# Two small-head attention stages: a new order of the steps, the maximum subtracted in float32, and no products with zeros

## The chip, the cores and the metric

The kernel runs on one core of a Trainium2 chip. Its time is the device time of one execution in microseconds (us). A core has five engines, each with its own queue, which it works through in order: TensorE (PE; its weight loads are listed as PEld), VectorE (DVE), ScalarE (ACT), GpSimd (POOL) and SyncE (SP), which here only issues DMAs. Engines wait for one another by semaphores.

## The reference

A residual stream `x` of 64 batches x 128 tokens x 128 dimensions passes eight stages: four times a cross attention over a context of 77 tokens x 64 dimensions and then a feed-forward part, each gated by a tanh. The change touches the attention of the layers 0 and 2, which both have 16 heads of dimension 8. Layer 2, shortened (layer 0 is the same without the biases):

```python
qh = (q @ Wq + bq).reshape(B, LQ, HEADS, D_K).transpose(0, 2, 1, 3)      # HEADS = 16, D_K = 8
kh = (k @ Wk + bk).reshape(B, LKV, HEADS, D_K).transpose(0, 2, 1, 3)
vh = (v @ Wv + bv).reshape(B, LKV, HEADS, D_K).transpose(0, 2, 1, 3)
scores = jnp.einsum('bhqd,bhkd->bhqk', qh, kh) * scale
attn = jax.nn.softmax(scores, axis=-1)
out = jnp.einsum('bhqk,bhkd->bhqd', attn, vh)
concat = out.transpose(0, 2, 1, 3).reshape(B, LQ, D_MODEL)
return concat @ Wo + bo
...
x = x + jnp.tanh(g_xattn[2]) * _L2_xattn_ref(_layernorm(x, axis=-1), ctx_512, ctx_512, ...)
```

## The kernel before

The stages run one after another. Both small-head attention stages come from one function, `small_head_attention`; their tiles begin with `l0x_` and `l2x_`. `x` stays on the core (`x_res`), and all 64 batches are worked on there, in 16 iterations of four batches.

**What an iteration does once for its four batches** ("front" steps): statistics and normalization of `x` (DVE, with the inverse deviation on POOL), the transposes of `x` (PE, L362), queries (PE, L712), keys (PE, L717), and the values of two batches at a time (`values`, 40 products, PE, L735). All of them write to one PSUM bank, `pa`, so each waits until the one before has been read: the queries by ACT (a 16-bit high part) and DVE (the remainder), the values by DVE (`block_values`, L953), which masks them into blocks.

**What it does for each batch j.** The 16 heads of 77 keys make 1232 columns of scores, in four groups of four heads. Half A holds two groups, half B the other two. For each half: `score` (PE, L747; three 16-bit products for high and low parts, each on two row groups of 32 rows, which write to two banks), `maximum` over the 77 keys of each head (DVE, L961), `split_max` (POOL, L676 and L678: the maximum as a high and a low bfloat16 part), `turn_max` (PE, L754: heads become rows), `fetch_max` (ACT, L878), `shift` (PE, L763: a product with a matrix of -1 that subtracts the maximum inside PSUM), `exponential` (ACT, L885). Then the probabilities are turned in ten chunks of 128 columns, in three units (four, four and two chunks): `turn` (PE, L778), `high` (ACT, L891), `rest` (DVE, L965), `weigh` (PE, L797: three products a chunk with the values; between two chunks one product of 368 columns with a tile of zeros, L801, into unused columns of the same bank). At last `divide` (DVE, L973 and L977), `turn_o` (PE, L807), a copy (ACT, L897), `output` (PE, L811) and `add` into `x` (DVE, L985).

**What sets the order.** Every engine has its own list of steps, written out by hand as one string for each of the four batches (a "slot"), for instance on PE

```python
fronts = ["v1 x", "q", "k", "v0"]
... "scoreA turn0 turn_o scoreB output " + f + " mtA turn1 weigh0 shiftA mtB turn2 shiftB weigh1 weigh2"
```

Each name has a pair of numbers: a lag in iterations, and how many slots ago its batch began (`ago`). So in the slot in which the scores of batch j are made, the probabilities of batch j-1 are turned and weighed, and batch j-2 is divided, turned and added. `turn1` waits for `add` of the batch before, since the output is written into the bank that its transposes need (`turned[1]`).

Two constants are made by POOL in the first block, before any stage: `piece_mask`, and `minus_one` with 32 selects of 77 columns, each waiting for the one before (`make_attention_constants`, L518).

Of the kernel before, what the change touches and what calls it, by code (L numbers as in the profile page):

```python
# [14 lines left out]
F32 = mybir.dt.float32  # L15
# [7 lines left out]
P = 128  # L23
# [475 lines left out]
def make_attention_constants(pool, g, s_made):  # L499
# [32 lines left out]
CONSTANTS = 2 + 10 + 32 + 10  # L532


def small_head_attention(nc, g, name, wq, wk, wv, wo, bq=None, bk=None, bv=None, bo=None, gate=0):
# [17 lines left out]
    with Stage(nc, name) as st:  # L553
# [3 lines left out]
        four, none, blank = st.sb("four", [P, 4], F16), st.sb("none", [P, 2, 4]), st.sb("blank", [P, BANK], F16)  # L557
# [6 lines left out]
        mx, mh, mT = st.sb2("mx", [P, 4, 4]), st.sb2("mh", [P, 4, 32], BF16), st.sb2("mT", [P, P], BF16)  # L564
# [15 lines left out]
        s_score, s_max, s_mh, s_ml, s_mt, s_mT, s_shift, s_exp = [  # L580
            st.sem(k) for k in ("s_score", "s_max", "s_mh", "s_ml", "s_mt", "s_mT", "s_shift", "s_exp")]
# [26 lines left out]
        with nc.Block() as block:  # L608
# [18 lines left out]
            def _(pool):  # L627
                for i in range(2):
                    for p in range(2):
                        pool.memset(v_lo[p][i][:, :, :, D:E1], 0.0).then_inc(s_set, 1)  # L630
                    pool.memset(mh[i][:, :, :], 0.0).then_inc(s_set, 1)
                pool.memset(none[:, :, :], 0.0).then_inc(s_set, 1)
                pool.memset(blank[:, :], 0.0).then_inc(s_set, 1)
                pool.wait_ge(s_set, 8)
                pool.sem_inc(s_set, 1)

                def context_rest(it):
# [4 lines left out]
                    if (due := nth(it, 8, 3, ago=1)) is not None:  # L642
                        pool.wait_ge(s_ml, due)
# [24 lines left out]
                def split_max(it, j, h):  # L668

                    p = j % 2  # L670
                    pool.wait_ge(s_max, nth(it, 8, 2 * j + h))
                    if (due := nth(it, 8, 2 * j + h, back=4)) is not None:
                        pool.wait_ge(s_mt, due)
                    m = mx[p][:, 2 * h:2 * h + 2, :]
                    high, low = mh[p][:, 2 * h:2 * h + 2, 0:4], mh[p][:, 2 * h:2 * h + 2, 4:8]
                    pool.tensor_tensor(high, m, none[:, :, :], ALU.add).then_inc(s_mh, 1)  # L676
                    pool.wait_ge(s_mh, nth(it, 8, 2 * j + h))
                    pool.tensor_tensor(low, m, high, ALU.subtract).then_inc(s_ml, 1)  # L678
# [15 lines left out]
                steps.update(one)  # L694
# [133 lines left out]
            def _(act):  # L828
# [14 lines left out]
                def fetch_x(it):  # L843
                    fr.fetch(act, it, s_q)
# [2175 lines left out]
```

## Time and profile before

| | |
|---|---|
| median of 3 runs | 6037.49 us (6032.2 to 6039.96) |
| the profiled execution | 6016.21 us, its span 6014.5 us |
| mean granted TensorE clock | 0.916 of full speed |
| busy in the span: PE / DVE / ACT / POOL | 4935.3 / 3921.6 / 2728.1 / 2172.3 us |
| l0x: first and last scores | 41.2 and 636.4 us |
| l2x: first and last scores | 2583.4 and 3181.3 us |
| L801, products with zeros, l0x and l2x | 576 each, busy 160.9 and 162.9 us |

The profile is of one execution. A row of a timeline gives the start, the duration and the shape of an instruction, or of a few like ones that follow each other; in brackets stands how long the engine was idle before it and who released it. Durations of matmuls include the time that a result takes through the array, so that two which follow each other overlap: what one costs on the engine is read from start to start. The granted clock is in parts of 2.4 GHz, and 0.5 is 1.2 GHz.

### The profile page before, as it was taken

Reading aid. Unit: us, or ns where it says so; the run is one execution under the profiler, and the core shown is the slowest. Engines: PE = TensorE matmul, PEld = TensorE weight load, DVE = VectorE, ACT = ScalarE, POOL = GpSimd, SP = SyncE. Lnnn points to the kernel's source line nnn. Section 1 sums busy time; section 2 is a strip of 40 time slices with the busy share of each in tenths; the row PEclk is TensorE's granted clock in tenths of the full one; section 3 lists DMA queues with packets and bytes.
Section 4 is the critical chain, followed back from the end, with each engine's and each line's share of the span. In section 5 each row is a group of like instructions: output and inputs, shape, how many; then the busy total and the mean of one; then the engine's idle time right before and its main releaser. Section 6 shows DMA issues by size and latency. Waiting matters only on the chain. (4 is left out here: it accounts for less than half of the span.)

```text
span 6014.5 us, 133734 instructions
## 1 busy us (share of the span) xinstructions
PE 4935.3 (82%) x41787; PEld 3611.9 (60%) x41787; DVE 3921.6 (65%) x9897; ACT 2728.1 (45%) x5454; POOL 2172.3 (36%) x3095
## 2 busy tenths in 40 slices
PE   6888898999962798078888998888898799998888
PEld 3555466888862465045555665776776577776544
DVE  4555585777766333245555776888887688888544
ACT  3444475555530233044444554555554355554344
POOL 4333100111117100733332334777775733333300
PEclk9999798999985899579997998999999899999988
DMA  1000500000011333100000000000000000000000
GB/s 37 5 4 3 242 0 14 5 5 5 5 49 43 115 135 115 50 10 5 4 3 12 1 0 9 0 0 0 0 0 5 7 2 2 2 2 6 1 11 18
DMA packets 108942, 140.25 MB, mean 23 GB/s; under 512 B 35832, under 2 KB 83256, under 8 KB 103996
## 3 DMA queue, kind: packets, MB, share of 16 engines
q1 hardware_dynamic: 100544, 120.88, 6.0%
q0 software_dynamic: 8192, 16.79, 1.0%
q8 instruction: 109, 1.79, 0.1%
q14 instruction: 97, 0.79, 0.0%
HBM read 47.44 MB, written 58.72 MB: 18 GB/s over the span
## 5 line engine op out<-in xcount | busy, mean ns | idle before, releaser
L2170 POOL TENSOR_TENSOR l3a_probs<-l3a_probs,l3a_later 128x512 f32<-128x512 f32 x256 | 320.7, 1281 | 4.9 <-DVE l3a_total L2358 4.9
L2156 POOL TENSOR_TENSOR l3a_keys<-l3a_kT,head 128x2048 f32<-128x2048 f32 x64 | 230.4, 3600 | 232.8 <-ACT l3a_kT L2283 232.8
L1585 POOL DMA_INDIRECT l1c_rows<-l_rows,l1f_slots x128 | 123.1, 961 | 442.5 <-PEq L1577 402.0
L2218 PE MATMUL l3a_scores<-l3a_keys,l3a_qT 128*128 128x512 f32 x512 | 255.1, 601 | 4.2 <-POOL l3a_keys L2156 4.2
L170 POOL TENSOR_TENSOR l1x_ve<-l1x_mv,eps 128x1 f32<-128x1 f32 x64 | 12.2, 190 | 657.6 <-DVE l1x_mv L162 657.6
L965 DVE SCALAR_TENSOR_TENSOR l0x_p_lo<-l0x_turned,l0x_p_hi 128x512 f16<-128x512 f32 (+1 forms) x192 | 115.7, 603 | 204.4 <-ACT l0x_p_hi L891 202.2
L298 PE MATMUL l3a_po<-l3a_vals,l3a_probsT 128*128 128x32 f32 x2048 | 248.0, 269 | 0.2
L965 DVE SCALAR_TENSOR_TENSOR l2x_p_lo<-l2x_turned,l2x_p_hi 128x512 f16<-128x512 f32 (+1 forms) x192 | 115.7, 603 | 202.8 <-ACT l2x_p_hi L891 200.6
L298 PEld LDWEIGHTS l3a_po<-l3a_vals,l3a_probsT 128*128 128x128 f32 x2048 | 246.8, 192 | 0.7 <-ACT l3a_probsT L279 0.4
L1656 POOL TENSOR_TENSOR l2f_hid<-l2f_prod,l2f_route 128x512 f32<-128x512 f32 x128 | 152.1, 1193 | 257.0 <-DVE l2f_prod L1803 253.7
L254 ACT ACTIVATE l3a_probs<-l3a_probs 128x512 f32<-128x512 f32 x256 | 161.7, 632 | 182.4 <-DVE l3a_probs L245 177.2
L1504 PE MATMUL l1e_h<-l1e_xhi,l1f_parts 128*128 128x512 f16 x640 | 204.4, 380 | 9.7 <-DVE l1e_gated L1562 8.2
L2156 POOL TENSOR_TENSOR l3c_keys<-l3c_kT,head 128x1232 f32<-128x1232 f32 x64 | 144.0, 2250 | 159.9 <-ACT l3c_kT L2283 159.9
L284 DVE SCALAR_TENSOR_TENSOR l1x_loT<-l1x_turned,l1x_hiT 77x512 f16<-77x512 f32 x256 | 168.7, 679 | 46.9 <-ACT l1x_hiT L277 46.8
L277 ACT ACTIVATE l3c_hiT<-l3c_turned 77x512 f16<-77x512 f32 x256 | 150.5, 588 | 106.8 <-PE l3c_po L298 104.3
L1097 ACT ACTIVATE l0f_relu<-l0f_h,l0f_route 128x512 f32<-128x512 f32 x256 | 158.0, 687 | 83.6 <-DVE l0f_route L1136 44.2
L2218 PE MATMUL l3c_scores<-l3c_keys,l3c_qT 128*128 128x308 f32 x512 | 191.8, 457 | 1.0 <-POOL l3c_keys L2156 1.0
L284 DVE SCALAR_TENSOR_TENSOR l3c_loT<-l3c_turned,l3c_hiT 77x512 f16<-77x512 f32 x256 | 173.7, 679 | 20.3 <-ACT l3c_hiT L277 20.3
L1562 DVE TENSOR_TENSOR l1e_gated<-l1e_h,l1e_silu 128x512 f32<-128x512 f32 x160 | 110.7, 692 | 114.7 <-ACT l1e_silu L1536 114.7
L279 ACT COPY l3a_probsT<-l3a_turned 128x512 f32<-128x512 f32 x256 | 150.3, 587 | 77.1 <-PE l3a_turned L266 76.8
L277 ACT ACTIVATE l1x_hiT<-l1x_turned 77x512 f16<-77x512 f32 x256 | 144.8, 590 | 86.0 <-PE l1x_po L298 76.7
L237 DVE TENSOR_REDUCE l3a_mx<-l3a_scores 128x4 f32<-128x512 f32 x256 | 169.8, 684 | 21.1 <-issue 16.6
(581 smaller groups left out, 17374.6 us busy)
## 6 DMA issues: line engine op xcount, KB each, us to landing
l_rows<-l0f_zeros SPq DMA_DIRECT2D x34, 1024.0 KB, 26.2
l1f_parts<-l1f_split SPq DMA_DIRECT2D x40, 512.0 KB, 3.6
l1e_x_in<-l_rows SPq DMA_DIRECT2D x40, 256.0 KB, 2.8
l1f_down<-l1f_w SPq DMA_DIRECT2D x40, 256.0 KB, 2.3
l_rows<-l1e_y_out SPq DMA_DIRECT2D x40, 256.0 KB, 2.7
l1f_w<-in_L_W SPq DMA_DIRECT2D x16, 256.0 KB, 3.4
out_x<-x_res SPq DMA_DIRECT2D x16, 256.0 KB, 2.0
x_res<-in_x SPq DMA_DIRECT2D x1, 3840.0 KB, 12.2
```

The costliest lines, as they stand in the source:

```text
L237: dve.tensor_reduce(self.mx[it.par][:, a:b], self.view(c), AX, ALU.max).then_inc(self.s_max, 1)
L254: act.activation(v, v, ACT.Exp, scale=self.scale).then_inc(self.s_exp, 1)
L277: act.activation(self.hiT[c % 2][:, :], src, ACT.Copy, scale=SPLIT_EXP).then_inc(self.s_fetch, 1)
L284: dve.scalar_tensor_tensor(self.loT[c % 2][:, :], self.ps_turn[c % 2][0:self.keys, :], SPLIT_EXP, self.hiT[c % 2][:, :], ALU.mult, ALU.sub ...
L298: last = pe.matmul(out_of(h), p[c % 2][:, cols], v, start=(i == 0), stop=(i == len(products) - 1))
L965: dve.scalar_tensor_tensor(p_lo[u][:, :], turned[u % 2][:, 0:len(UNITS[u]) * P], SPLIT_EXP, p_hi[u][:, :], ALU.mult, ALU.subtract).then_in ...
L1097: act.activation(relu[e][:, :], ps_h[e][:, :], ACT.Relu, scale=rt.w[it.par][:, j, e:e + 1]).then_inc(s_relu, 1)
L1504: last = pe.matmul(bank[:, :], parts[p][:, w, f], x[p][:, :], start=(k == 0), stop=(k == 2))
L1656: pool.tensor_tensor(hid[k % 2][:, :].rearrange("p (e m) -> p e m", m=M), prod[k % 2][:, :].rearrange("p (e m) -> p e m", m=M), rt.w[it.pa ...
L2156: pool.tensor_tensor(keys[it.par][:, :, :, :], kT[it.par][:, :, :].unsqueeze(2).to_broadcast([P, J, G4, T]), g.head32[:, :].unsqueeze(1).u ...
L2170: pool.tensor_tensor(v, v, later[:, :].unsqueeze(1).to_broadcast([P, 4, T]), ALU.mult).then_inc(s_masked, 1)
L2218: pe.matmul(scores[c][:, 0:G4 * T], qT[it.par][:, c, :], keys[it.par][:, c, :, :].rearrange("p h t -> p (h t)"), start=True, stop=True).th ...
```

## The change

- **Order.** A batch now takes two slots and no third: the transposes of its first unit stand in the slot of its scores (`turn0`, `ago` 0), its other units, the division, `turn_o`, `output` and `add` in the next one (`ago` 1). The front steps move to the slot's end, and the second values block (`v1`) to the middle of the fourth slot, before `turn_o`; the transposes of `x` stand at that slot's end, and some front steps run one iteration earlier than before.
- **Maximum.** `split_max` goes. DVE writes the maximum into a float32 tile of 32 columns a group, whose others are zero; `turn_max` and `shift` are float32 products, and `mT` and `minus_one` are float32.
- **Zeros.** The products with zeros (L801) and their tile go.
- **Constants.** `minus_one` needs 16 selects in place of 32, and both constants are made in the block of l0x, by POOL, after it has cleared its tiles. A copy of the identity in bfloat16 goes.

```diff
-    for k in range(8):
-        part, j = k // 4, k % 4
+    for j in range(4):
         v = g.minus_one[:, j, :]
         for q in range(4):
-            pool.affine_select(out=v, in_=v, compare_op=ALU.not_equal, fill=-1.0, base=-(32 * q + 4 * part + j),
+            pool.affine_select(out=v, in_=v, compare_op=ALU.not_equal, fill=-1.0, base=-(32 * q + j),
...
-        mx, mh, mT = st.sb2("mx", [P, 4, 4]), st.sb2("mh", [P, 4, 32], BF16), st.sb2("mT", [P, P], BF16)
+        mx, mT = st.sb2("mx", [P, 4, 32]), st.sb2("mT", [P, P])
...
+                if first_use:
+                    make_attention_constants(pool, g, g.s_made)
...
-                def split_max(it, j, h):
...
-                skewed(pool, n, slots(steps, ["maxA value1 maxB s1", "maxA maxB rest s2 " + ("bias" if biased else ""),
-                                              "maxA maxB deviation s3", "maxA maxB next value0"]), 6)
+                skewed(pool, n, slots(steps, ["s1 value0", "deviation s2 value1", "s3 " + ("bias" if biased else ""), "next rest"]), 6)
...
-                    pe.wait_ge(s_ml, nth(it, 8, 2 * j + h))
-                    pe.matmul(scores[h][64 * h:64 * h + 64, W + 12:W + 12 + P], mh[j % 2][:, 2 * h:2 * h + 2, :].rearrange("p g r -> p (g r)"),
-                              g.ident16[:, :], start=False, stop=True, skip_group_check=True).then_inc(s_mt, 1)
+                    pe.wait_ge(s_max, nth(it, 8, 2 * j + h))
+                    pe.matmul(scores[h][64 * h:64 * h + 64, W + 12:W + 12 + P], mx[j % 2][:, 2 * h:2 * h + 2, :].rearrange("p g r -> p (g r)"),
+                              g.ident[:, :], start=False, stop=True, skip_group_check=True).then_inc(s_mt, 1)
...
-                        if c < 9:
-
-                            pe.matmul(po[:, HEADS * E1:BANK], blank[:, 0:P], blank[:, HEADS * E1:BANK], start=False, stop=False,
-                                      skip_group_check=True)
...
-                    steps[f"turn{u}"] = (lambda it, j, u=u: turn(it, j, u), 2, 1)
+                    steps[f"turn{u}"] = (lambda it, j, u=u: turn(it, j, u), 2, 1 if u else 0)
                     steps[f"weigh{u}"] = (lambda it, j, u=u: weigh(it, j, u), 2, 1)
-                fronts = ["v1 x", "q", "k", "v0"]
-                skewed(pe, n, slots(steps, ["scoreA turn0 turn_o scoreB output " + f + " mtA turn1 weigh0 shiftA mtB turn2 shiftB weigh1 weigh2"
-                                            for f in fronts]), 6)
+                fronts = [("", "q"), ("", "k"), ("", "v0"), ("v1", "x")]
+                skewed(pe, n, slots(steps, ["scoreA turn1 turn2 weigh0 mtA weigh1 shiftA weigh2 scoreB turn0 " + mid +
+                                            " turn_o mtB output shiftB " + end for mid, end in fronts]), 6)
...
-                fronts = ["v1 x", "c q", "k", "v0"]
-                skewed(act, n, slots(steps, ["o high0 " + f + " mA high1 expA mB high2 expB" for f in fronts]), 6)
+                fronts = [("x", "v0"), ("q", "v1"), ("k", ""), ("", "c")]
+                skewed(act, n, slots(steps, [begin + " high1 high2 mA expA " + mid + " high0 o mB expB" for begin, mid in fronts]), 6)
...
-                dve.tensor_reduce(mx[j % 2][:, 2 * h:2 * h + 2, :], half(h), AX, ALU.max).then_inc(s_max, 1)
+                dve.tensor_reduce(mx[j % 2][:, 2 * h:2 * h + 2, 0:4], half(h), AX, ALU.max).then_inc(s_max, 1)
...
-                fronts = ["norm v1", "q", "k stats", "v0"]
-                skewed(dve, n, slots(steps, ["divide maxA rest0 maxB add " + f + " rest1 rest2" for f in fronts]), 6)
+                fronts = [("", "", "stats"), ("q", "", "norm"), ("k", "", ""), ("v0", "v1", "")]
+                skewed(dve, n, slots(steps, ["maxA rest1 rest2 " + begin + " maxB divide rest0 " + mid + " add " + end
+                                             for begin, mid, end in fronts]), 6)
```

On PE, before the change, the second half of a slot of l0x with the keys, from the output product to the second subtraction (`mh` is the split maximum, `mT` the turned one, `po` the weighed values):

```order
L811 MATMUL l0x_turned<-l0x_wo,l0x_oT 128x128 [waits l0x_s_oT]
L717 MATMUL l0x_pa<-l0x_ctx,l0x_wk 128x308 [waits l0x_s_qlo,l0x_s_ctx0]
L754 MATMUL l0x_scores<-ident,l0x_mh 64x128 [waits l0x_s_ml]
L778 MATMUL l0x_turned<-ident,l0x_probs 128x128 [waits l0x_s_x,l0x_s_exp]
...
L797 MATMUL l0x_po<-l0x_v_hi,l0x_p_hi 128x18 [waits l0x_s_o,l0x_s_vlo,l0x_s_lo]
...
L801 MATMUL l0x_po<-l0x_blank 128x368
...
L763 MATMUL l0x_scores<-minus_one,l0x_mT 128x308 [waits l0x_s_mT]
L763 MATMUL l0x_scores<-minus_one,l0x_mT 128x308
L754 MATMUL l0x_scores<-ident,l0x_mh 64x128 [waits l0x_s_ml]
L778 MATMUL l0x_turned<-ident,l0x_probs 128x128 [waits l0x_s_lo,l0x_s_exp]
...
L763 MATMUL l0x_scores<-minus_one,l0x_mT 128x308 [waits l0x_s_mT]
```

After it, PE in the corresponding stretch, from the scores of half B to the keys at the slot's end (`mx` is the maximum in float32, `o` the divided result):

```order
L730 MATMUL l0x_scores<-l0x_keys_hi,l0x_q_hi 128x308 [waits l0x_s_exp,l0x_s_keys]
...
L761 MATMUL l0x_turned<-ident,l0x_probs 128x128 [waits l0x_s_lo,l0x_s_exp]
...
L786 MATMUL l0x_turned<-ident,l0x_o 128x128 [waits l0x_s_o]
L737 MATMUL l0x_scores<-ident,l0x_mx 64x128 [waits l0x_s_max]
L790 MATMUL l0x_turned<-l0x_wo,l0x_oT 128x128 [waits l0x_s_oT]
L746 MATMUL l0x_scores<-minus_one,l0x_mT 128x308 [waits l0x_s_mT]
L746 MATMUL l0x_scores<-minus_one,l0x_mT 128x308
L700 MATMUL l0x_pa<-l0x_ctx,l0x_wk 128x308 [waits l0x_s_qlo,l0x_s_ctx0]
```

The division's transpose and the output have moved between the two halves' subtractions, the keys behind the second one, and the turned maximum waits for VectorE itself (`s_max`) and no longer for GpSimd (`s_ml`).

On DVE, before the change, one slot with the keys (`mx` maximum, `p_lo` remainder of the probabilities, `recip` and `o` the division):

```order
L973 RECIPROCAL l0x_recip<-l0x_po 128x16 [waits l0x_s_o,l0x_s_weigh]
L977 TENSOR_TENSOR l0x_o<-l0x_po,l0x_recip 128x128 [waits l0x_s_oTp,l0x_s_recip]
L961 TENSOR_REDUCE l0x_mx<-l0x_scores 128x8 [waits l0x_s_ml,l0x_s_score]
L965 SCALAR_TENSOR_TENSOR l0x_p_lo<-l0x_turned,l0x_p_hi 128x512 [waits l0x_s_hi]
L961 TENSOR_REDUCE l0x_mx<-l0x_scores 128x8 [waits l0x_s_ml,l0x_s_score]
L985 SCALAR_TENSOR_TENSOR x_res<-l0x_turned,gates,x_res 128x128 [waits l0x_s_y]
L944 TENSOR_TENSOR l0x_k_lo<-l0x_pa,l0x_k_hi 128x308 [waits l0x_s_khi]
```

And after it, the slot that takes up the keys:

```order
L942 TENSOR_REDUCE l0x_mx<-l0x_scores 128x2x4 [waits l0x_s_mt,l0x_s_score]
L946 SCALAR_TENSOR_TENSOR l0x_p_lo<-l0x_turned,l0x_p_hi 128x512 [waits l0x_s_hi]
L946 SCALAR_TENSOR_TENSOR l0x_p_lo<-l0x_turned,l0x_p_hi 128x256 [waits l0x_s_hi]
L923 TENSOR_TENSOR l0x_k_lo<-l0x_pa,l0x_k_hi 128x308 [waits l0x_s_khi]
L942 TENSOR_REDUCE l0x_mx<-l0x_scores 128x2x4 [waits l0x_s_mt,l0x_s_score]
L954 RECIPROCAL l0x_recip<-l0x_po 128x16 [waits l0x_s_o,l0x_s_weigh]
L958 TENSOR_TENSOR l0x_o<-l0x_po,l0x_recip 128x128 [waits l0x_s_oTp,l0x_s_recip]
L946 SCALAR_TENSOR_TENSOR l0x_p_lo<-l0x_turned,l0x_p_hi 128x512 [waits l0x_s_hi]
L966 SCALAR_TENSOR_TENSOR x_res<-l0x_turned,gates,x_res 128x128 [waits l0x_s_y]
```

The division stood ahead of both maxima and now stands behind the second.

## Rows read from the trace of the kernel before

**Rows 1.** Windows: length; busy us of PE, PEld, DVE, ACT, POOL; granted clock; DMA; GB/s.

```profile
315.07:352.35 37.28, 30.58 (x373) 19.72 (x370) 20.76 (x50) 17.61 (x38) 13.68 (x29) 0.95 0.02 4
...
308.60:312.00 3.40, 3.40 (x25) 2.31 (x24) 0.57 (x1) 1.59 (x4) 2.74 (x5) 0.54 0.00 0
...
609.00:636.00 27.00, 25.03 (x176) 13.74 (x175) 9.67 (x20) 8.37 (x19) 5.00 (x14) 0.50 0.00 1
```

**Rows 2.** Timeline, PE, one slot: start, duration, what, [idle before <- releaser].

```profile
315.07 0.30 PE L747 MATMUL l0x_scores<-l0x_keys_hi,l0x_q_hi 32*128 32x308 f16 x2
...
315.57 0.66 PE L778 MATMUL l0x_turned<-ident,l0x_probs 128*128 128x128 f32 x4
...
316.76 0.49 PE L811 MATMUL l0x_turned<-l0x_wo,l0x_oT 128*128 128x128 f32 x2
317.08 1.02 PE L712 MATMUL l0x_pa<-l0x_xT,l0x_wq 128*128 128x512 f32 x2
318.04 0.24 PE L754 MATMUL l0x_scores<-ident,l0x_mh 128*64 128x128 bf16 x1
318.97 0.63 PE L778 MATMUL l0x_turned<-ident,l0x_probs 128*128 128x128 f32 x4 [0.69 <-DVE x_res L985]
...
321.83 0.30 PE L763 MATMUL l0x_scores<-minus_one,l0x_mT 32*128 32x308 bf16 x2 [0.53 <-ACT l0x_mT L878]
...
323.39 0.30 PE L747 MATMUL l0x_scores<-l0x_keys_hi,l0x_q_hi 32*128 32x308 f16 x2
```

**Rows 3.** Timeline, PE, end of the iteration's fourth slot.

```profile
345.63 0.93 PE L362 MATMUL l0x_pa<-ident,l0x_xn 128*128 128x128 f32 x4 [2.37 <-DVE l0x_v_f L953]
...
352.35 0.30 PE L747 MATMUL l0x_scores<-l0x_keys_hi,l0x_q_hi 32*128 32x308 f16 x2
```

**Rows 4.** Timeline, DVE, the slot of rows 2.

```profile
315.18 0.26 DVE L973 RECIPROCAL l0x_recip<-l0x_po 128x16 f32<-128x16 f32 x1 [0.86 <-PE l0x_po L797]
315.47 0.29 DVE L977 TENSOR_TENSOR l0x_o<-l0x_po,l0x_recip 128x128 f32<-128x128 f32 x1
315.76 0.80 DVE L961 TENSOR_REDUCE l0x_mx<-l0x_scores 128x8 f32<-128x616 f32 x1
...
320.34 0.69 DVE L965 SCALAR_TENSOR_TENSOR l0x_p_lo<-l0x_turned,l0x_p_hi 128x512 f16<-128x512 f32 x1 [0.81 <-ACT l0x_p_hi L891]
```

**Rows 5.** Timeline, POOL, the slot of rows 2.

```profile
316.73 0.20 POOL L676 TENSOR_TENSOR l0x_mh<-l0x_mx,l0x_none 128x8 bf16<-128x8 f32 x1 [4.90 <-DVE l0x_mx L961]
317.00 0.20 POOL L678 TENSOR_TENSOR l0x_mh<-l0x_mx,l0x_mh 128x8 bf16<-128x8 f32 x1
```

**Rows 6.** Timeline, ACT, the slot of rows 2.

```profile
319.71 0.60 ACT L891 ACTIVATE l0x_p_hi<-l0x_turned 128x512 f16<-128x512 f32 x1 [0.75 <-PE l0x_turned L778]
...
321.51 0.26 ACT L878 CAST l0x_mT<-l0x_scores 64x128 bf16<-64x128 f32 x1
...
322.17 0.68 ACT L885 ACTIVATE l0x_probs<-l0x_scores 128x616 f32<-128x616 f32 x1
```

**Rows 7.** Timeline, PE, weighing: a zero product and what follows.

```profile
319.51 0.32 PE L801 MATMUL l0x_po<-l0x_blank 128*128 128x368 f16 x1
319.67 0.17 PE L797 MATMUL l0x_po<-l0x_v_hi,l0x_p_hi 128*128 128x27 f16 x1
319.69 0.17 PE L797 MATMUL l0x_po<-l0x_v_lo,l0x_p_hi 128*128 128x27 f16 x1
```

**Rows 8.** Timeline, PE, two float32 products of 308 columns, elsewhere.

```profile
325.50 0.78 PE L717 MATMUL l0x_pa<-l0x_ctx,l0x_wk 64*128 64x308 f32 x2
...
4855.05 0.68 PE L2218 MATMUL l3c_scores<-l3c_keys,l3c_qT 128*128 128x308 f32 x2
```

**Rows 9.** Timeline, ACT and POOL, start of the kernel.

```profile
4.34 0.21 ACT L2911 ACTIVATE gates<-gates_in 128x8 f32<-128x8 f32 x1 [2.24 <-DMA gates_in<-in_g_ffn]
4.85 6.22 POOL L518 TENSOR_SCALAR_AFFINE_SELECT minus_one<-minus_one 128x77 bf16<-128x77 bf16 x16
...
26.88 0.20 POOL L339 TENSOR_TENSOR l0x_ve<-l0x_mv,eps 128x4 f32<-128x4 f32 x1 [4.75 <-DVE l0x_mv L329]
```

More of the change, by code:

```diff
@@ L529, in make_attention_constants @@
     return n
-CONSTANTS = 2 + 10 + 32 + 10
+CONSTANTS = 2 + 10 + 16 + 10
 def small_head_attention(nc, g, name, wq, wk, wv, wo, bq=None, bk=None, bv=None, bo=None, gate=0):
@@ L556, in small_head_attention @@
         bqkv_s, bo_s, bvo_s = st.sb("bqkv", [P, 3]), st.sb("bo", [P, P]), st.sb("bvo", [P, P])
-        four, none, blank = st.sb("four", [P, 4], F16), st.sb("none", [P, 2, 4]), st.sb("blank", [P, BANK], F16)
+        four = st.sb("four", [P, 4], F16)
         ctx2, ctxT = st.sb2("ctx2", [P, GROUP, KEYS]), st.sb2("ctxT", [P, GROUP, 3, KEYS], F16)
@@ L641, in context_rest @@
                     pool.wait_ge(fr.s_rstd, nth(it))
-                    if (due := nth(it, 8, 3, ago=1)) is not None:
-                        pool.wait_ge(s_ml, due)
+                    if (due := nth(it, 4, 0, ago=1)) is not None:
+                        pool.wait_ge(s_keys, due)
                     lo = ctxT[p][CTX:P, :, :, :]
@@ L666, in value_rest @@
                                        ALU.subtract).then_inc(s_vlo, 1)
-                def split_max(it, j, h):
[L670 to L678, printed above, removed]
                 def add_bias(it):
@@ L686, in add_bias @@
                     pool.tensor_tensor(x, x, bvo_s[:, :].unsqueeze(1).to_broadcast([P, GROUP, P]), ALU.add).then_inc(s_bo, 1)
-                steps = {"maxA": (lambda it, j: split_max(it, j, 0), 2, 0), "maxB": (lambda it, j: split_max(it, j, 1), 2, 0)}
-                one = {"deviation": (lambda it, j: fr.inverse_deviation(pool, it), 0, 0), "rest": (lambda it, j: context_rest(it), 1, 0),
-                       "bias": (lambda it, j: add_bias(it), 1, 0), "value0": (lambda it, j: value_rest(it, 0), 1, 0),
+                steps = {"deviation": (lambda it, j: fr.inverse_deviation(pool, it), 0, 0), "rest": (lambda it, j: context_rest(it), 0, 0),
+                       "bias": (lambda it, j: add_bias(it), 1, 0), "value0": (lambda it, j: value_rest(it, 0), 2, 0),
                        "value1": (lambda it, j: value_rest(it, 1), 2, 0), "next": (lambda it, j: spread(it, 0), 1, 0),
@@ L811, in output @@
                     pe.matmul(y_p, oT[j % 2][:, :], wo_s[:, :], start=True, stop=True).then_inc(s_y, 1)
-                steps = {"x": (lambda it, j: turn_x(it), 1, 0), "q": (lambda it, j: queries(it), 1, 0), "k": (lambda it, j: keys_of(it), 1, 0),
-                         "v0": (lambda it, j: values(it, 0), 1, 0), "v1": (lambda it, j: values(it, 1), 2, 0),
-                         "turn_o": (turn_o, 2, 2), "output": (output, 2, 2)}
+                steps = {"x": (lambda it, j: turn_x(it), 0, 0), "q": (lambda it, j: queries(it), 1, 0), "k": (lambda it, j: keys_of(it), 1, 0),
+                         "v0": (lambda it, j: values(it, 0), 1, 0), "v1": (lambda it, j: values(it, 1), 1, 0),
+                         "turn_o": (turn_o, 2, 1), "output": (output, 2, 1)}
                 for h, half_name in enumerate("AB"):
@@ L905, in _ @@
                 for u in range(3):
-                    steps[f"high{u}"] = (lambda it, j, u=u: high(it, j, u), 2, 1)
-                fronts = ["v1 x", "c q", "k", "v0"]
-                skewed(act, n, slots(steps, ["o high0 " + f + " mA high1 expA mB high2 expB" for f in fronts]), 6)
+                    steps[f"high{u}"] = (lambda it, j, u=u: high(it, j, u), 2, 1 if u else 0)
+                fronts = [("x", "v0"), ("q", "v1"), ("k", ""), ("", "c")]
+                skewed(act, n, slots(steps, [begin + " high1 high2 mA expA " + mid + " high0 o mB expB" for begin, mid in fronts]), 6)
             @block.vector
```

34 lines of the change are left out of this document (14 added, 20 removed).

## The prediction

> **What bounds the kernel now.** I read the page's table of slices first, then the windows of one iteration, then the timelines of the four engines for one slot. The change touches only the two small-head attention stages, l0x and l2x. Each walks 64 batches in groups of four; a batch is one slot of the order, and four slots make an iteration. One iteration of l0x takes 37.28 us, in which TensorE is busy 30.58, VectorE 20.76, ScalarE 17.61 and GpSimd 13.68 [rows 1]. No engine is full: TensorE is nearest, but a good part of its time is the products with zeros and pipeline overlap. What sets the slot is therefore a ring of hand-overs, and the PE timeline of a slot shows it [rows 2]: scores of one half at 315.07, transposes of the previous batch, output, query product at 317.08, the turned maximum at 318.04, then 0.69 us of idleness until VectorE's residual add lets the transposes at 318.97 go, later 0.53 us for the maximum copied by ScalarE, and the next slot at 323.39: 8.32 us. Three slots of an iteration are like that, the fourth is longer: from the row at 345.63, where TensorE has just stood idle 2.37 us for the value products to leave the shared bank, to the next slot at 352.35 [rows 3]; 37.28 less three times about 8.35 leaves 12.2 us for it. That hole has a second price: right behind the same hole of the iteration before, from 308.60 to 312.00, the granted clock is 0.54, against 0.95 over a whole iteration [rows 1], so the work behind the hole runs at the lower of the two levels, 1.2 and not 2.4 GHz.
>
> Between score and subtraction a half passes VectorE (maximum 0.80 us [rows 4]), GpSimd (two instructions of 0.20, 0.27 apart [rows 5]), TensorE (0.24 [rows 2]), ScalarE (0.26 [rows 6]) and TensorE again (0.30 [rows 2]).
>
> **Part 1, products with zeros.** Nine go per batch. One moves the next product on by 0.16 us, from 319.51 to 319.67, and a value product moves it by 0.02 to 0.03 [rows 7]. So 9 x 0.16 = 1.4 us per slot leave TensorE. In the old order they stand between the wait and the next slot, so they are on its ring; this is the surest gain, 1.4 x 128 slots = 180 us if nothing took its place. The float32 steps below take most of it.
>
> **Part 2, the maximum in float32.** GpSimd's two steps go, 0.20 + 0.27 and a hand-over, some 0.5 us per half. In their place the turn becomes a float32 product of 128 columns: the output product has this form and takes 0.49 us for its two instructions [rows 2], against 0.24, so +0.25. The subtraction is the term that decides. Now two products of 308 columns in different row groups finish together in 0.30 us [rows 2]. In float32 each is two instructions; the nearest rows are a float32 pair of 308 columns on 64 rows, 0.78 us, and one on the whole array, 0.68 [rows 8]. No row has two of them in neighbouring row groups. Lower bound: they overlap wholly, 0.70 us. Upper bound: one after the other, 1.2 to 1.4 us. Since a product's two instructions are issued one behind the other in the same row group, only the second of the first product can run beside the first of the second product, which makes three instructions' time in place of four: 3 x 0.26 and some 0.12 for entering the 32-row form. I take 0.90 us of issue. There are 256 such steps (2 halves x 128 batches), so 0.1 us on each is 26 us of the total.
>
> The Trainium skill ("TensorE: Matmul & The Clock Gate", Part 3) says that products in distinct row groups run concurrently, about 4 ns apart. The trace agrees for 16-bit operands (the 0.30 above). By that rule read for whole products the step would be 0.70; read for instructions in program order, 0.90. No run here shows it for float32.
>
> **Part 3, the order.** I lay out a new slot by its order, with the rows' durations. Scores A: 0.50 (315.07 to 315.57 [rows 2]). The second chunk of the previous batch is then turned, copied high, subtracted and weighed: 0.66 for four transposes [rows 2], 0.63 from the copy's start to the remainder's, 0.69 for the remainder [rows 4, 6], with 0.12 of hand-overs 2.10. Beside it lie the third chunk's transposes, the first chunk's weighing, the maximum of half A (0.80, ready 1.5 us into the slot) and its turn: they cost nothing, but that stands on the 2.10; without this cover the maximum's way would be 0.80 + 0.49 + 0.26. Weighing chunk 1: 12 products, 0.31. Subtraction A: 0.90. Weighing chunk 2: 0.15. Scores B until VectorE can start, 0.61, and their maximum, 0.80; the division that is now queued behind that maximum on VectorE: 0.58 (0.26 and 0.29 with a gap [rows 4]); hand-over 0.10; together 2.10. The exponential of A (0.68 [rows 6]) and the transposes of chunk 0 lie beside this. Turning o 0.15, turning maximum B 0.49, its copy 0.26, hand-overs 0.12: 1.02. Subtraction B: 0.90. Sum 0.50 + 2.10 + 0.31 + 0.90 + 0.15 + 2.10 + 1.02 + 0.90 = 7.98 us. Behind it comes the slot's front step: queries 0.96 (317.08 to 318.04 [rows 2]), keys 0.70 (0.78 [rows 8] less the end that overlaps), values 40 x 0.026 = 1.04, and in the last slot the transposes of x, 0.50, with about 0.25 more for the second values block, of whose 1.04 the rest fits into the wait for the division. The front also hides the exponential of B: 0.90 + 0.96 + 0.50 is longer than the way from subtraction B through 0.68 us of exponential.
>
> So the four slots are 8.94, 8.68, 9.02 and 8.73: 35.4 us against 37.28. The three ordinary slots get longer by 0.5 (the ring now holds two subtractions in float32 and the division behind a maximum), the long one shorter by 3.5: the wait for the values bank goes, since the second values block stands early in its slot with three steps between it and x's transposes, and with it the spell of low clock. 1.9 us x 32 iterations = 61 us. Other edits cost nothing: GpSimd's queue is shorter by 16 short steps an iteration, so each wait that it served ends no later; the ScalarE copy of the maximum has the same size; the context load keeps two iterations of lead.
>
> **Part 4, the start.** Sixteen of the 32 selects that make the constants go. Sixteen take 6.22 us [rows 9]. The rest moves from the first block into l0x, ahead of GpSimd's first work on the deviation, which now starts at 26.88 [rows 9]. The first block then lasts only until the gates are made, 4.55 [rows 9], and what leaving it takes, an estimated 6 us; clearing takes about 2; of the constants 6.2 for the sixteen selects and an estimated 3.5 for the others remain (in float32, which I take to cost the same). So GpSimd is free at about 17.7, and the weights, now requested while the large load of x is under way, land at about the same time. Gain 9 us, between 6 (only the selects) and 12.
>
> **The sum.** 61 + 9 = 70 us off the profiled execution's 6016.2 us (span 6014.5 and 1.7 around it): 5946. The median of the runs is 6037.5, 21 above; with the same 70 it becomes 5967 us.
>
> **Rivals.**
> A. The two subtractions overlap wholly (0.70): 0.2 x 256 = 51 us more, 5916; with looser hand-overs than I reckon, down to 5870. For it: 16-bit products do overlap [rows 2]. Against: the issue order within a product. Chance 0.22.
> B. They do not overlap (1.2 to 1.4): 84 us or more are lost, 6050 to 6095, no change or slightly slower. For it: float32 on 64 rows already takes 0.10 more than on the whole array [rows 8]. Chance 0.14.
> C. The slower side: the clock. Without zero products the ordinary slots have thinner work, and if TensorE is granted 1.2 GHz there, its terms on the path double: scores 1.0, first transposes 0.5, weighing 0.46, subtractions 1.8, turn 0.3, front 0.85, that is 4.9 us per slot, 627 us if it held for all 128. The point from which it decides is a ninth of the slots beyond what runs low today; at a third of the slots the time is about 5967 + 209 = 6176. For it: the last 27 us of l0x, which have no front steps but still the zero products, run at 0.50 clock [rows 1]. Against: today's falls follow a hole of 2.4 us, and the longest wait that I find in the new slot is 0.8; and the float32 turns and subtractions put back 0.25 and 0.6 us of work per half, more than the 1.4 us of zeros per slot. Chance 0.13.
> The Trainium skill (same page, Part 4) says that transposes do not count as busy for the clock gate. By that rule only the stretch between scores A and subtraction A would be thin, which is rival C.
>
> **How the numbers follow.** Forecast 0.51, its own range 5925 to 6010; A 0.22; B 0.14; C 0.13. A measurement of this kernel can tell about 0.2%, 12 us, from no change. Faster by more: forecast, A and a little of B, 0.77. Within 0.2%: a part of B, 0.07. Slower: the rest of B and C, 0.16. The range takes in A and the lower end of B: 5855 to 6055.
>
> **What would show it.** Right: an iteration of about 35.4 us with four nearly equal slots; no idleness over 1 us before the transposes of x; subtraction steps at a pace of 0.9; the first deviation at 18 us; clock at or above 0.95 in both stages. Wrong: a step of 0.70 or 1.2 in its place (A, B), VectorE's division no longer the last thing before o's turn, a granted clock of 0.5 over whole slots (C), or a wait of TensorE for GpSimd's keys.

## The result and the profile after

The changed kernel takes 6371.4 us (median; 6370.8 to 6376.8) against 6037.6 (6032.2 to 6040.0): a ratio of 1.055, 95% interval 1.0534 to 1.0566. It is slower by 334 us where 70 fewer were forecast; 404 us lie between, about two thirds of the 627 that rival C, the clock, had for all slots. Rival C is what happened.

The page of the changed kernel: span, busy times, and TensorE's granted clock in 40 slices.

```profile
span 6369.6 us, 131931 instructions
PE 5431.0 (85%) x41403; PEld 3838.7 (60%) x41403; DVE 3933.8 (62%) x9897; ACT 2733.7 (43%) x5454; POOL 2067.6 (32%) x2562
PEclk8555589899995799555555799999999899999978
```

The two groups of fives are the two stages. Windows of the changed kernel, with the columns of [rows 1]: a slot, four slots, and most of each stage.

```profile
314.89:327.33 12.44, 12.39 (x114) 7.80 (x112) 5.38 (x12) 4.47 (x9) 3.22 (x3) 0.50 0.01 1
302.87:351.56 48.69, 46.63 (x358) 26.77 (x358) 20.95 (x50) 17.89 (x38) 10.57 (x13) 0.54 0.02 4
100.00:600.00 500.00, 483.16 (x3599) 276.12 (x3599) 213.69 (x510) 182.32 (x388) 108.15 (x133) 0.52 0.02 4
2800.00:3300.00 500.00, 484.01 (x3654) 277.11 (x3650) 215.73 (x510) 184.32 (x388) 121.28 (x143) 0.51 0.02 4
```

An iteration takes 48.69 us where [rows 1] has 37.28 and the forecast 35.4. TensorE is busy 46.63 us of it and is now the bound, at 1.2 GHz: the ring of hand-overs has become a full engine. (48.69 - 37.28) x 32 = 365 us, and the start gives 6 back: about the 355 us by which the spans of the two profiled executions differ (6369.6 and 6014.5). The timeline of PE shows one slot, and in the next one a short return to 2.4 GHz.

```profile
327.33 0.44 PE L730 MATMUL l0x_scores<-l0x_keys_hi,l0x_q_hi 32*128 32x308 f16 x2
...
330.00 0.69 PE L737 MATMUL l0x_scores<-ident,l0x_mx 128*64 128x128 f32 x2
...
331.25 1.39 PE L746 MATMUL l0x_scores<-minus_one,l0x_mT 32*128 32x308 f32 x4
332.58 0.20 PE L780 MATMUL l0x_po<-l0x_v_hi,l0x_p_hi 128*128 128x18 f16 x1
...
333.72 1.11 PE L761 MATMUL l0x_turned<-ident,l0x_probs 128*128 128x128 f32 x4
335.26 0.48 PE L786 MATMUL l0x_turned<-ident,l0x_o 128*128 128x128 f32 x1 [0.43 <-DVE l0x_o L958]
335.67 0.69 PE L737 MATMUL l0x_scores<-ident,l0x_mx 128*64 128x128 f32 x2
336.29 0.80 PE L790 MATMUL l0x_turned<-l0x_wo,l0x_oT 128*128 128x128 f32 x2
337.02 1.40 PE L746 MATMUL l0x_scores<-minus_one,l0x_mT 32*128 32x308 f32 x4
338.35 2.08 PE L695 MATMUL l0x_pa<-l0x_xT,l0x_wq 128*128 128x512 f32 x2
340.35 0.44 PE L730 MATMUL l0x_scores<-l0x_keys_hi,l0x_q_hi 32*128 32x308 f16 x2
...
343.01 0.43 PE L737 MATMUL l0x_scores<-ident,l0x_mx 128*64 128x128 f32 x2
...
344.24 0.79 PE L746 MATMUL l0x_scores<-minus_one,l0x_mT 32*128 32x308 f32 x4
344.96 0.18 PE L780 MATMUL l0x_po<-l0x_v_hi,l0x_p_hi 128*128 128x18 f16 x1
...
347.15 0.48 PE L786 MATMUL l0x_turned<-ident,l0x_o 128*128 128x128 f32 x1 [0.61 <-DVE l0x_o L958]
```

The start of one instruction to the start of the next is its pace. A subtraction has 1.33 us (331.25 to 332.58) at 1.2 GHz and 0.72 (344.24 to 344.96) at 2.4; queries 2.00 (338.35 to 340.35) where [rows 2] has 0.96. The longest wait in this piece is 0.61 us, for the division; from 100 to 600 us it is 0.7 (us in all, times, longest):

```profile
PE l0x_turned L786 <- DVE l0x_o L958: 11.9, 31, 0.7
```

So the clock lies at 1.2 GHz although TensorE is 96% busy and never waits 1 us.

### The profile page after: what moved, and what is told of

Read it like the earlier page. It is cut to its first block and busy times, and to the rows that moved or that the text cites. A ratio compares the mean times of both kernels' runs of the same rounds, so it can differ in the third digit from the quotient of the medians.

```text
span 6369.6 us, 131931 instructions
## 1 busy us (share of the span) xinstructions
PE 5431.0 (85%) x41403; PEld 3838.7 (60%) x41403; DVE 3933.8 (62%) x9897; ACT 2733.7 (43%) x5454; POOL 2067.6 (32%) x2562
## 5 line engine op out<-in xcount | busy, mean ns | idle before, releaser
L942 DVE TENSOR_REDUCE l0x_mx<-l0x_scores 128x8 f32<-128x616 f32 x128 | 102.4, 800 | 306.7 <-PE l0x_scores L730 306.7
L942 DVE TENSOR_REDUCE l2x_mx<-l2x_scores 128x8 f32<-128x616 f32 x128 | 102.4, 800 | 302.2 <-PE l2x_scores L730 302.2
L864 ACT ACTIVATE l0x_probs<-l0x_scores 128x616 f32<-128x616 f32 x128 | 87.5, 683 | 217.1 <-PE l0x_scores L746 217.1
## 6 DMA issues: line engine op xcount, KB each, us to landing
x_res<-in_x SPq DMA_DIRECT2D x1, 3840.0 KB, 12.4
```

The source lines that it names most:

```text
L942: dve.tensor_reduce(mx[j % 2][:, 2 * h:2 * h + 2, 0:4], half(h), AX, ALU.max).then_inc(s_max, 1)
```

## The experiments

The ratio is to runs of the kernel before on the same chip, and its interval is 0.1 to 0.4% to either side; times of different chips are compared by the ratios where it matters. "Clock" is the granted clock from 100 to 600 us, inside l0x. "Split" is the maximum as two bfloat16 parts made by GpSimd, as before; "direct" one bfloat16 value written by VectorE.

| run | order | maximum | zeros in weighing | in the wait | us | ratio | clock |
|---|---|---|---|---|---|---|---|
| before | old | split | 9 | 0 | 6037.6 | 1 | 0.94 |
| e2 | old | split | 0 | 0 | 6073.3 | 1.0071 | 0.59 |
| e6 | old | split | 9, on 32 rows | 0 | 6581.7 | 1.0922 | 0.55 |
| e4 | new | split | 9 | 0 | 6028.7 | 0.9986 | 0.87 |
| e5 | new | split | 0 | 0 | 6104.9 | 1.0129 | 0.52 |
| e3 | old | float32 | 9 | 0 | 6238.7 | 1.0346 | 0.89 |
| e16 | old | float32 | 0 | 0 | 6211.1 | 1.0287 | 0.62 |
| e1 | new | float32 | 9 | 0 | 6216.5 | 1.0301 | 0.83 |
| after | new | float32 | 0 | 0 | 6371.4 | 1.0550 | 0.52 |
| e7 | new | float32 turn, bfloat16 subtraction | 0 | 0 | 6103.2 | 1.0130 | 0.54 |
| e9 | new | float32 | 9 | 4 | 6089.4 | 1.0067 | 0.97 |
| e10 | new | float32 | 0 | 4 | 6134.7 | 1.0134 | 0.69 |
| e14 | new | float32 | 0 | 4, on 32 rows | 6510.9 | 1.0774 | 0.51 |
| e13 | old | direct | 9 | 0 | 6027.4 | 0.9986 | 0.93 |
| e8 | new | direct | 9 | 0 | 6002.0 | 0.9955 | 0.86 |
| e11 | new | direct | 9 | 4 | 5933.6 | 0.9808 | 0.97 |
| e12 | new | direct | 0 | 4 | 6029.2 | 0.9979 | 0.70 |
| e15 | new | direct | 5 | 5 | 5891.0 | 0.9750 | 0.95 |

### Three parts, one at a time (e1 to e5, e16)

**e1**: the changed kernel with the zero products back in `weigh`.

```diff
+                        if c < 9:
+                            pe.matmul(po[:, HEADS * E1:BANK], blank[:, 0:P], blank[:, HEADS * E1:BANK], start=False, stop=False, ...)
```

> The changed kernel with the products with zeros put back between the chunks, nothing else. Theory 1 (clock: the zeros held TensorE's clock up): granted clock in both stages back to 0.9 or more, an iteration of 36 to 39 us instead of 48.7, time 6000 to 6100 us. Theory 2 (float32: the turn and the subtraction in float32 are too long for the ring, whatever the clock): the zeros only add 1.4 us a slot, time 6400 us or more, clock as low as in the changed kernel.

**e2**: the kernel before without these two lines.

> The kernel before without the products with zeros, nothing else. Theory 1: the clock falls to 0.5 for most of both stages and the slots go from 8.3 to 10 us or more, time above 6200 us. Theory 2: the ring gets shorter by 1.4 us a slot, 1.4 x 128 = 180 us, time about 5860 us, clock above 0.85 there.

**e3**: the old order and its zeros, the maximum in float32 (`mx`, `mT`, `minus_one` and the turn as in the change, and the constants made in l0x).

> The old order with the products with zeros, but with the float32 maximum (no GpSimd step, float32 turn and subtraction) and the constants made in l0x. Theory 1: clock at 0.9 or more in both stages; on the ring 2 x (0.25 + 0.6) are added and 2 x 0.5 go, about 0.7 us a slot, 6037 + 90 - 6 = 6120 us. Theory 2: 6300 us or more.

**e4**: the new order with the zeros and `split_max` of before. The constants are made in l0x, but with all 32 selects, so nothing is gained at the start (first scores at 41.6 us).

> The new order with the old maximum (split by GpSimd, bfloat16 turn and subtraction) and with the products with zeros. Theory 1: clock 0.9 or more, the ring is that of e1 less the float32 parts (2 x 0.85) plus GpSimd (2 x 0.5), an iteration of 34 to 37 us, time 5930 to 6040 us. Theory 3 (the order itself is what is longer, since the division stands behind the second maximum): 6050 us or more at a clock of 0.9.

**e5**: e4 without the zeros.

> The new order, with the maximum split into two bfloat16 parts by GpSimd as before and without the products with zeros. It completes the square of order, type of the maximum, and zeros. Theory 1 (taking the zeros out costs through the clock, by an amount that grows with the float32 work that then runs at 1.2 GHz): 6029 for the new order with zeros, plus about the 34 us that their removal cost in the old order: 6055 to 6090, stage clock 0.55 to 0.65. Rival 1 (the new order itself is too thin for the clock, the type does not matter): plus the 155 us of the float32 pair, about 6180. Rival 2 (in the new order the zeros are on the ring and their 1.4 us a slot come back): below 5950.

**e16**: e3 without the zeros.

> The old order with the maximum in float32 and without zeros: the missing corner. If type and zeros are all (float32 subtractions on 32 rows do not hold the clock and take 1.33 us at 1.2 GHz against 0.37): 6239 with zeros plus about the same 155 as in the new order: 6340 to 6420, stage clock 0.50 to 0.55. Rival (the new order makes the fall, the old one keeps 1.0 in its ordinary slots as with bfloat16): 6239 + 35 = 6260 to 6290.

With the zeros in, the order is worth -9 us (split) and -22 (float32), and float32 costs 201 (old) and 188 (new). The -9 is not clear of nothing: e4's interval is 0.9973 to 1.0. Taking the zeros out costs 36 and 76 with the split maximum (43 and 86 by the ratios), but -28 in the old order and +155 in the new one with float32 (-36 and +150 by the ratios; the -36 has an interval of some 29 to either side).

Of the expectations only e4's was met, and its clock, 0.87, was under the 0.9 expected. e1 (6216) and e2 (6073) fell between their two theories, e3 (6239) between its 6120 and its 6300, and e5 (6105, clock 0.52) between 6090 and its rival's 6180. In e2 the clock did fall as theory 1 had it, to 0.59, but the time rose by 36 us only. The parts do not add: in e16 I expected 6340 to 6420 and its rival 6260 to 6290, and both failed. One thing in e3 explains a piece of it. The waits of PE there, from 100 to 600 us:

```profile
PE l0x_scores L731 <- issue: 15.4, 8, 3.1
```

Eight stops of up to 3.1 us in which nothing that the profile shows is awaited; neither the kernel before nor e16 has such a row among its waits there. Over two stages of 700 us that is some 40 us of e3's 6239, and more with the fall of the clock behind them: a slot of 9.3 us without a stop lasts 12.4 to 13.7 with one. What these stops are was not tried. Without them, taking the zeros out would cost the old order some 12 us or more in place of saving 28, and in the new order it costs 155. The clock says the same: without zeros it is 0.59 and 0.62 in the old order, 0.52 in the new one, with either type.

### Turn or subtraction (e7)

```diff
-        mx, mT = st.sb2("mx", [P, 4, 32]), st.sb2("mT", [P, P])
+        mx, mT = st.sb2("mx", [P, 4, 32]), st.sb2("mT", [P, P], BF16)
```

and `minus_one` in bfloat16.

> The changed kernel with its products with zeros back, the turn of the maximum in float32, but the turned maximum copied and subtracted as one bfloat16 product. Theory (the float32 steps cost what they add to TensorE's work, since with zeros TensorE is nearly full): the turn adds 0.25 us and the subtraction 0.45 to each of 256 halves, so of the 187 us between the split bfloat16 maximum (6029) and float32 (6216) some 64 stay: 6029 + 64 = 6093, less up to 30 if GpSimd's two steps were on the ring; 6060 to 6100. Rival (it is the turn, with its two loads of a weight that was just written, that costs): about 6200. Rival (only the clock matters and 16-bit subtractions keep it): 6030 or less.

This text says that the zeros are back, but the kernel that ran has none, so its expectation was not put to the test, and it stands beside e5 and the changed kernel. 6103.2 against 6104.9: a float32 turn without GpSimd's two steps costs what the split cost, within the 6 us by which e7's first scores come earlier (35.6 and 41.6). All that lies between e7 and the changed kernel, 268 us (254 by the ratios), is the subtraction in float32, at nearly the same clock (0.54 and 0.52): 256 steps x (1.33 - 0.37) = 246 us, with 0.37 us as the pace of the bfloat16 one in e7 at 1.2 GHz (both rows are of e7, timeline of PE):

```profile
300.77 0.44 PE L746 MATMUL l0x_scores<-minus_one,l0x_mT 32*128 32x308 bf16 x2
301.14 1.39 PE L700 MATMUL l0x_pa<-l0x_ctx,l0x_wk 64*128 64x308 f32 x2
```

### What holds the clock (e6, e9, e10, e14)

**e6**: the kernel before, its zeros on 32 rows.

```diff
-  pe.matmul(po[:, HEADS * E1:BANK], blank[:, 0:P], blank[:, HEADS * E1:BANK], ...)
+  pe.matmul(po[:, HEADS * E1:BANK], blank[0:32, 0:P], blank[0:32, HEADS * E1:BANK], ...)
```

> The kernel before, with its products with zeros on 32 rows of the array in place of 128; same count, columns and places in the order. If what holds the clock is that TensorE is streaming, whatever the rows: the time of before, 6025 to 6050, clock 0.91. If rows in use count, the zeros on 32 rows hold it no better than none: clock near 0.85 as without zeros, and since their 1.4 us a slot are still spent and at the lower clock count double, 6150 to 6300.

The clock fell from 0.94 to 0.55 with the same number of columns streamed, so it is not streaming as such that holds it. The time went beyond my range, since a product on 32 rows between products on 128 costs more than its columns. A chunk (three value products, one of zeros) of e6:

```profile
304.37 0.22 PE L797 MATMUL l0x_po<-l0x_v_hi,l0x_p_hi 128*128 128x18 f16 x1
304.44 0.18 PE L797 MATMUL l0x_po<-l0x_v_lo,l0x_p_hi 128*128 128x18 f16 x1
304.47 0.17 PE L797 MATMUL l0x_po<-l0x_v_hi,l0x_p_lo 128*128 128x18 f16 x1
304.57 0.48 PE L801 MATMUL l0x_po<-l0x_blank 32*128 32x368 f16 x1
304.99 0.20 PE L797 MATMUL l0x_po<-l0x_v_hi,l0x_p_hi 128*128 128x27 f16 x1
```

0.62 us (304.37 to 304.99), where the same chunk of the kernel before in its spell at 1.2 GHz has 0.39:

```profile
310.56 0.22 PE L797 MATMUL l0x_po<-l0x_v_hi,l0x_p_hi 128*128 128x18 f16 x1
310.69 0.47 PE L801 MATMUL l0x_po<-l0x_blank 128*128 128x368 f16 x1
310.95 0.23 PE L797 MATMUL l0x_po<-l0x_v_hi,l0x_p_hi 128*128 128x27 f16 x1
```

0.23 x 9 x 128 = 265 us of e6 are that.

**e9, e10 and e14** put four zero products where TensorE waits for the division (0.43 to 0.80 us), into a bank that is free then: e9 on top of e1, e10 on the changed kernel alone, e14 as e10 with `blank[0:32, ...]`.

```diff
                 def turn_o(it, j):
+                    for _ in range(4):
+                        pe.matmul(turned[1][:, 0:368], blank[:, 0:P], blank[:, 0:368], start=True, stop=True)
                     pe.wait_ge(s_o, nth(it, 4, j))
```

> The new order with float32 maximum and its products with zeros back, and four more products with zeros (128 rows, 368 columns, 0.16 us each at 2.4 GHz) placed where TensorE waits 0.8 us for the division, before the turn of o. They write a part of a PSUM bank that is free then. Theory (the clock is the cause of the slots beyond 9.17 us, and it is held by products on all 128 rows): the granted clock in the stages rises from 0.83 towards 0.95, an iteration comes to 4 x 9.2 = 37 us in place of 43, and the time to 6010 to 6060. Rival (TensorE was full, so more products only lengthen the ring): 6216 plus 4 x 0.16 x 128 = 82 at most, 6220 to 6300.

> The changed kernel as it is, with only the four products with zeros in the wait before the turn of o, none among the value products. If four such products in the wait are enough to keep 2.4 GHz, the layout of the forecast can be read: an iteration of 35.4 to 36.5 us and a time of 5965 to 6010. If they are not enough, they cost at 1.2 GHz 4 x 0.31 less the wait of 0.5: about 0.7 us a slot, 6371 + 90 = 6460; between the two if the clock comes back for some slots. I expect the latter, 6200 to 6460, since 0.65 us of them is less than half the 1.4 us that were taken out.

> The kernel of the run with four zeros in the wait alone (6135; the changed kernel 6371), with these four on 32 rows in place of 128: same columns, same place. If any streaming holds the clock: 6120 to 6160, stage clock 0.69 to 0.74. If only rows in use count: the clock stays at 0.50 to 0.53 and the four cost what they take beyond the wait at 1.2 GHz, 6420 to 6500.

Work added, time gone: e1 6216 to e9 6089, the changed kernel 6371 to e10 6135. On 32 rows the same four cost 376 us more than on 128. None of the three expectations was met in time. e9 is 29 us above its range; its stops of up to 3.1 us with no releaser, 11.8 and 11.0 us in 500 us of either stage, are about that much. e10 is faster than the 6200 that I had as its lower end. e14 is 11 us above 6500, since the four took 1.34 us with the change from and to products on 128 rows, where I had 1.24, and filled a wait of 0.29 us a slot on average (11.9 us in 500 us of the changed kernel), where I had 0.5. PE windows (length, PE busy, granted clock, DMA share, GB/s) from 100 to 600 us, of e10 (the profiled execution took 6210 us, where three of its five took 6121 to 6135), then of e14:

```profile
100.00:600.00 500.00, 480.17 (x4162) 0.69 0.02 4
```

```profile
100.00:600.00 500.00, 495.62 (x3471) 0.51 0.02 4
```

e14 is the busier of the two and stays at 1.2 GHz. In this kernel four products a slot on all 128 rows raise the clock; the same products on 32 rows do not. It fits that the float32 subtractions, 0.72 us of 32-row products per half, did not stand in for the zeros: e7, which has them in bfloat16, has 0.54 where the changed kernel has 0.52.

### Towards a better version (e8, e11, e12, e13, e15)

**e8**: the new order with zeros, and VectorE writes the maximum straight as bfloat16. The same rounded value is subtracted from all keys of a query and head, so it cancels in the softmax.

```diff
-        mx, mT = st.sb2("mx", [P, 4, 32]), st.sb2("mT", [P, P])
+        mx, mT = st.sb2("mx", [P, 4, 32], BF16), st.sb2("mT", [P, P], BF16)
```

> The new order with zeros; VectorE writes the maximum straight as one bfloat16 value, GpSimd takes no part, turn and subtraction stay in bfloat16. The same value is subtracted from all keys of a query and head, so it cancels in the softmax. If GpSimd's two steps and hand-overs (0.5 us a half) are on the ring of the new order: up to 0.5 x 256 = 128 us below the 6029 of the same order with the split: 5900 to 5960. If they lie beside TensorE's other work: 6010 to 6030.

**e11**: e8 with the four products in the wait. **e12**: e11 without the zeros in `weigh`. **e13**: e8's edit in the old order. **e15**: e11 with `if c < 9 and c % 2 == 0` (five zeros in weighing) and `range(5)`.

> The new order, the maximum as one bfloat16 value without GpSimd, the zeros among the value products, and the four in the wait before the turn of o. Without the four, slots at a clock of 1.00 last 8.22 to 8.74 us and the slots with the keys and the values 10.9 at 0.69. Theory (the fill holds the clock through those): 34 us an iteration against 37, 3 x 32 = 96 below 6002: 5890 to 5930, stage clock 0.95 or more. Rival (the spell at 1.2 GHz comes from the keys' float32 product on 64 rows, not from the wait): no change or slower, 6000 to 6060.

> The same with the four in the wait alone, none among the value products. Where the wait is the thin place, the clock holds and the 1.4 us a slot are gone from the ring: 5850 to 5890. Where the amount over the slot counts, four are too few for nine: stage clock 0.5 to 0.7 and 6050 to 6120, as the same order without zeros (6105).

> The old order with its zeros, the maximum as one bfloat16 value written by VectorE, no GpSimd step (constants made in l0x as in the changed kernel). In the old order TensorE waits some 0.5 us for the turned maximum, behind GpSimd's two steps. If that wait goes with them, without another in its place: 0.3 to 0.5 us in half of the steps, 40 to 60 us, and 6 of the start: 5975 to 5995, as good as the new order (6002), so that the order is worth nothing. Rival (the ring in the old order runs over the residual add, not the maximum): 6020 to 6040, and the direct maximum pays only in the new order.

> The best version so far (5934) with five zeros among the value products in place of nine, and five in the wait in place of four. If the wait was the thin place, the clock stays at 0.95 or more and some 0.6 us a slot less stand on TensorE, of which about half on the ring: 0.3 x 128 = 40 us, 5890 to 5910. If the amount over the slot counts: stage clock 0.8 to 0.9 and 5960 to 6010.

GpSimd's two steps lie beside other work: nothing measurable in the old order (e13, interval 0.997 to 1.0003, as its rival had it), 0.3% in the new one (e8 against e4, each by its ratio), of which 6 us, a third, is the earlier start (first scores at 35.7 and 41.6 us). e8 fell between its two ranges. The four in the wait bring 68 us (e8 to e11; 89 by the ratios), 4 us above the range, at the clock expected. In e12 the four alone do not suffice (clock 0.70, and 6029 us, between its two ranges). e15 is the best kernel here: 0.975 of before, interval 0.973 to 0.9769, as its first theory had it. PE windows by slot, from one turn of o to the next, of e11 and of e15:

```profile
338.63:347.92 9.29, 9.01 (x154) 1.00 0.00 0
347.92:356.06 8.14, 7.67 (x80) 1.00 0.00 0
356.06:364.73 8.67, 8.13 (x77) 1.00 0.00 0
364.73:373.04 8.31, 7.78 (x77) 1.00 0.08 19
```

```profile
301.72:309.62 7.90, 7.18 (x77) 1.00 0.00 0
309.62:318.04 8.42, 7.64 (x75) 1.00 0.00 0
318.04:326.03 7.99, 7.29 (x74) 1.00 0.08 20
326.03:335.96 9.93, 9.75 (x152) 0.83 0.00 0
```

34.4 us in e11's iteration and 34.2 in e15's, against 37.28. At the same clock four zeros fewer in weighing (one more in the wait) shorten a slot by 0.24 to 0.32 us, about half of their 0.64. In the iteration of e15 shown here the slot with both value blocks falls to 0.83 and gives most of that back. In about half of e15's iterations it does not fall and lasts 9.1 us, and over l0x, from the first scores to the last, e15 takes 532 us and e11 552; l2x gives 22 us more, together about the 43 us between the two runs.

The place counts beside the number, as e15 and e8 suggest: ten zero products a slot, five of them in the wait, give a clock of 0.95, and nine, none in the wait, give 0.86. No run adds four elsewhere than in the wait, so how much is due to the place is not shown.

## Why the prediction was wrong

**The step that failed** is the weighing of rival C: "the float32 turns and subtractions put back 0.25 and 0.6 us of work per half, more than the 1.4 us of zeros per slot". I counted busy time. The larger part, the subtractions, are products on 32 rows, and e14 against e10 shows that such products do not hold the clock (0.51 against 0.69); of what was put back only the turns' 0.25 us run on 128 rows. For the same reason part 1 priced the zeros at 1.4 us per slot and at nothing otherwise. My other argument against C, that a fall needs a long wait, was wrong too: the fall in the kernel before does follow a hole of 2.4 us [rows 3], but the clock of the changed kernel is 0.50 over whole slots, and its longest wait from 100 to 600 us is 0.7 us. The row that spoke for C, the last 27 us of l0x at 0.50 with TensorE 25.03 us busy [rows 1], was the one to follow: busy and slow at once. And once TensorE is full, the price is no longer the terms on the ring but all its work. C's 4.9 us per slot was an overestimate all the same: an iteration is longer than the forecast by 13.3 us, 3.3 a slot. Of the 1.6 us between, 0.9 is the subtraction, which C doubles from 0.90 to 1.80 us where it takes 1.33, twice a slot; the rest was not taken apart.

How the 404 us between forecast and result divide, two experiments show: with the zeros back (e1) 155 us go, and with the clock at 0.97 (e9) another 127. The 122 us left down to the forecast's 5967 are about what nine zero products a slot make at half their time (0.7 us x 128 = 90) with e9's stops (some 29).

**Part 1.** Removal at a constant clock is worth half its time (e11, e15), not 1.4 us per slot. With what the clock does, removal costs 36 to 155 us except in the old order with float32.

**Part 2.** The turn: 0.43 us in its row against 0.24, forecast +0.25; about right in size, and nearly free (e7). The subtraction: 0.72 at 2.4 GHz, not 0.90. Rival A's number, 0.70, was right and my argument from the issue order wrong: both pairs overlap. (The prediction's 0.12 for entering the 32-row form has no row there; 2 x 0.72 - 1.33 = 0.11 is the part of the step that does not grow when the clock halves.) GpSimd's 0.5 us per half was off the ring. The sum does not rest on it, but my expectations of e3 and e4 gave credit for it, wrongly. At a clock of 1.00, float32 makes slots of

```profile
307.80:316.94 9.14, 8.94 (x87) 1.00 0.00 0
316.94:326.57 9.63, 9.46 (x82) 1.00 0.01 2
326.57:335.88 9.31, 9.06 (x82) 1.00 0.10 19
```

(e9, PE windows) against 8.14, 8.67 and 8.31 for the same slots of e11: 1.0 us more per slot. Neither kernel has GpSimd's steps, so my terms make 2 x (0.25 + 0.60) = 1.7 us; the step was 0.49 us longer than in bfloat16 and not 0.60: 0.72 against 0.23 from start to start, the latter from 321.83 [rows 2] to

```profile
322.06 0.19 PE L797 MATMUL l0x_po<-l0x_v_hi,l0x_p_hi 128*128 128x27 f16 x1
```

How much of the rest lay beside waits was not taken apart.

**Part 3.** The layout was near. e9's three slots and the one before them, with both value blocks,

```profile
297.52:307.80 10.28, 10.28 (x160) 1.00 0.01 3
```

make an iteration of 38.4 us (297.52 to 335.88). Take half of nine zeros from each (0.7 us): 35.6, against 35.4 forecast. This is worked out; no run shows the order with float32, no zeros and a full clock. The nearest, e10, has iterations in l0x from 37.5 us, at clocks of 0.84 to 1.00, to 47.9. The wait for the values bank did go, and with it the hole. What the layout missed is that a gain of the order holds only at 2.4 GHz: with zeros in weighing alone the order brings 0.14%, at a clock of 0.87 (e4). That it is its own wait for the division which lets the clock sink is likely, since zeros put there bring it back (e8 to e11), but not shown apart from their number. The division was the last thing before o's turn, as forecast.

**Part 4.** GpSimd starts on l0x at 6.04 us and on the deviation at 18.25, as forecast (18). But the first scores come at 35.5 in place of 41.2: 5.7 us, just under the range of 6 to 12. In the old order with the same constants (e3, e13) they come at 32.5, 8.7 us earlier: the constants gave the 9 us, and the new order's own start takes 3 of them back.

**Still open:** why without zeros the old order holds 0.59 to 0.62 and the new one 0.52. The new order sets transposes and weighing, the 128-row work, between the 32-row steps in smaller portions; that this is the reason is argued, not shown. Nor does any run separate the transposes, which also run on all rows, from the value products: whether both help to hold the clock is not known.

## What to carry to other kernels

Before you remove "useless" products from TensorE, or put others in their place, compare the rows of the array that they use, not only their time: with 32-row products among its work the engine was 96 to 99% busy here, at half the clock. Price a fall of the clock by all the work of TensorE, since the engine may become the bound. And look for a wait that already exists: four to five full-row products placed there gave back 68 to 237 us, while those among the value products cost half their time (e11, e15).

## What the runs showed of the hardware

- Granted clock 0.51 with TensorE 99% busy (e14), 0.69 with the same columns on 128 rows (e10), and 0.97 with nine more such products a slot (e9).
- Two float32 products of 308 columns on neighbouring groups of 32 rows, two instructions each, take 0.72 us together at 2.4 GHz and 1.33 at 1.2, about the 0.68 to 0.78 of a single one [rows 8].
- A 32-row product of 368 columns between 128-row products lengthens a chunk from 0.39 to 0.62 us at 1.2 GHz (e6).
- Two kernels with both float32 steps and zeros show stops of up to 3.5 us on TensorE with no releaser (in 500 us of l0x and of l2x: 8 and 4 in e3, 4 and 4 in e9); a third such kernel, e1, shows none. They were not looked into.
